# Perceiver block on one NeuronCore: all four P·V tiles of a batch in one slot, four buffers of transposed P, one of keys

## What is computed

```
ln = _ln(latents, g_l, b_l);  xn = _ln(x, g_x, b_x)          # latents 16x64x512, x = context 16x512x512
q = ln @ w_q
k, v = split(concat([xn, ln], axis=1) @ w_kv)                # 576 keys and values per batch
sim = einsum('bhid,bhjd->bhij', q * scale, k)                # 8 heads of 64
attn = softmax(where(mask, sim, -max))                       # P
out = einsum('bhij,bhjd->bhid', attn, v)                     # P·V
return _ln(out @ w_out, g_o, b_o)
```

## Time and profile before

| | us |
|---|---|
| three runs | 958.75, 959.94, 959.97 |
| median | 959.94 |
| the profiled execution | 958.88 |
| its span, first to last instruction | 957.1 |

### The profile page before, as it was taken

How to read it: one execution, slowest core, us unless ns; L and a number is a source line. 1 busy time by engine, 2 the same in 40 slices (tenths; PEclk the granted TensorE clock), 3 DMA queues, 4 the chain that set the end, 5 groups by cost and what they waited for, 6 DMA issues and landing times.

```text
span 957.1 us, 16824 instructions
## 1 busy us (share of the span) xinstructions
PE 942.2 (98%) x6400; PEld 777.4 (81%) x6400; DVE 730.1 (76%) x1512; ACT 522.4 (55%) x1088; POOL 142.7 (15%) x175
## 2 busy tenths in 40 slices
PE   9999999999999999999999999999999999999997
PEld 8778888888888888888888888776776778888885
DVE  6636577788787887886886854778898788999985
ACT  4535777777687777777776874623343422222221
POOL 6420101101201210111012010132231100000000
PEclk9999999999999999999999999999999999999999
DMA  6687657655675565676567535090004940000000
GB/s 223 167 280 209 200 135 192 158 130 157 166 185 131 163 152 154 155 196 149 129 147 181 157 106 161 12 242 2 1 1 118 247 121 12 11 12 12 12 12 23
DMA packets 119453, 120.07 MB, mean 125 GB/s; under 512 B 47430, under 2 KB 88070, under 8 KB 117324
## 3 DMA queue, kind: packets, MB, share of 16 engines
q1 hardware_dynamic: 111980, 93.30, 37.3%
q0 software_dynamic: 6816, 24.64, 8.3%
q10 hardware_dynamic: 576, 1.05, 0.3%
HBM read 89.04 MB, written 29.93 MB: 124 GB/s over the span
## 4 chain that ended last, share of the span: by engine, by line
PE 85%; DVE 6%; ACT 4%; DMA 2%; SPq 1%; issue 1%; POOL 0%; DVEq 0%; ACTq 0%; POOLq 0%
PE ps_banks L147 21%; PE ps_banks L148 21%; PE ps_banks L149 21%; PE ps_banks L473 6%; PE ps_banks L605 4%; PE ps_banks L686 3%; PE ps_banks L755 2%; PE ps_banks L756 2%; PE ps_banks L757 2%; SPq L132 1%; DMA sb_w_out_raw<-in_w_out 1%; DMA sb_wdn<-scratch_wdn 1%; PE ps_banks L486 1%; PE ps_banks L589 1%; PE ps_banks L651 1%
## 5 line engine op out<-in xcount | busy, mean ns | idle before, releaser
L147 PE MATMUL ps_banks<-sb_zT_hi,sb_wkv_hi 128*128 128x512 f32 x256 | 104.7, 409 | 0.0
L148 PE MATMUL ps_banks<-sb_wkv_lo,sb_zT_hi 128*128 128x512 f32 x256 | 100.4, 392 | 0.0
L147 PE MATMUL ps_banks<-sb_wkv_hi,sb_zT_hi 128*128 128x512 f32 x256 | 100.4, 392 | 0.0
L149 PE MATMUL ps_banks<-sb_zT_hi,sb_wkv_lo 128*128 128x512 f32 x256 | 100.3, 392 | 0.0
L149 PE MATMUL ps_banks<-sb_wkv_hi,sb_zT_lo 128*128 128x512 f32 x256 | 100.0, 391 | 0.0
L148 PE MATMUL ps_banks<-sb_zT_lo,sb_wkv_hi 128*128 128x512 f32 x256 | 99.9, 390 | 0.0
L987 DVE CUSTOM_DVE_ANT_0 sb_probs<-ps_banks,sb_maskbias 128x576 f32<-128x576 f32 x64 | 48.2, 754 | 41.5 <-PE ps_banks L149 39.9
L936 DVE TENSOR_TENSOR sb_kfull<-ps_banks,sb_rstd_row 128x512 f32<-128x512 f32 x64 | 44.2, 690 | 44.2 <-PE ps_banks L149 44.2
L1466 ACT ACTIVATE sb_kT_hi<-sb_kfull 128x512 fp32r<-128x512 f32 x64 | 40.5, 632 | 65.2 <-DVE sb_kfull L936 64.4
L147 PE MATMUL ps_banks<-sb_wgu,sb_z_hi 128*128 128x512 f32 (+1 forms) x192 | 74.0, 385 | 0.0
L148 PE MATMUL ps_banks<-sb_wgu,sb_z_hi 128*128 128x512 f32 (+1 forms) x192 | 72.1, 376 | 0.0
(11 more groups left out here) (275 smaller groups left out, 2520.8 us busy)
## 6 DMA issues: line engine op xcount, KB each, us to landing
sb_ctx<-in_ctx SPq DMA_DIRECT2D x16, 1024.0 KB, 6.4
sb_ctxT<-in_ctx_t SPq DMA_DIRECT2D x16, 1024.0 KB, 6.1
scratch_wgu<-sb_w_both POOLq DMA_DIRECT2D x22, 512.0 KB, 5.5
sb_wgu<-scratch_wgu SPq DMA_DIRECT2D x44, 256.0 KB, 5.0
sb_wdn<-scratch_wdn SPq DMA_DIRECT2D x8, 704.0 KB, 8.5
scratch_q<-sb_a_qk POOLq DMA_DIRECT2D x8, 512.0 KB, 6.6
sb_rstd_row<-scratch_rstd SPq DMA_DIRECT2D x16, 256.0 KB, 4.3
sb_qpack<-scratch_q SPq DMA_DIRECT2D x32, 128.0 KB, 6.2
```

Source lines behind the costliest of these rows:

```text
L147: e.matmul(o, wh, xh, start=i == 0, stop=False)
L148: e.matmul(o, wh, xl, start=False, stop=False)
L149: m = e.matmul(o, wl, xh, start=False, stop=i == n - 1)
```

## The change

- `weigh_v` of all four tiles of a batch stands in slot 3 of the next batch; slot 0 has none. In the last turn, b = 16, it is the same.
- Transposed P gets four buffers, one for each tile, in place of two: `p_main[n]` for the 512 context keys and `p_latent[n]` for the latents. `copy_p(b, n)` waits for `weigh_v(b - 1, n)` in place of the tile two before it. The ones in the latents' buffers are set four times at the start, not twice.
- `k_full` has one buffer. `scale_k` of a tile waits until `lo_of_k` of the tile ahead of it is done, not of the one before that. Both are DVE's.
- `w_q4` loses its own buffer: the rounded weights are written over `quant_w[3]` (`xn`, step 3's result). So step 3 of a job waits until the job ahead has been turned; before, the last step did.
- Two sets of statistics share their first tile with others, and two tiles of the self attention (`y[1]` and a gap of 2048 bytes) change places.

```
-                    if old and slot == 0:
-                        weigh_v(b - 1, 0)
-                        weigh_v(b - 1, 1)
                     if old and slot == 3:
-                        weigh_v(b - 1, 2)
-                        weigh_v(b - 1, 3)
+                        for n in range(C):
+                            weigh_v(b - 1, n)
...
+                        p = p_latent[n][:, r] if k == CS else p_main[n][:, k, r]
+                        m = e.matmul(o_space(r, n), value, p, start=k == CS, stop=k == CS - 1)
...
-                if idx >= 2:
-                    on.wait_ge(k_split, idx - 1)
-                e.tensor_tensor(k_full[n % 2][:, :], psum[:, bank, :], rstd_row[:, :], ALU.mult).then_inc(drained[bank])
+                if idx:
+                    on.wait_ge(k_split, idx)
+                e.tensor_tensor(k_full[:, :], psum[:, bank, :], rstd_row[:, :], ALU.mult).then_inc(drained[bank])
...
-                        if step == QUANT_STEPS - 1 and job:
+                        if step == 3 and job:
                             taken(("w", job - 1))
...
-                if idx >= 2:
-                    on.wait_ge(v_weighed, idx - 1)
-                copy(p_t[j][:, 0:CS, :].rearrange("p c n -> p (c n)"), psum[:, bank, :], drained[bank])
+                if b:
+                    on.wait_ge(v_weighed, C * (b - 1) + n + 1)
+                copy(p_main[n].rearrange("p c n -> p (c n)"), psum[:, bank, :], drained[bank])
...
+        w_q4 = quant_w[3]
-        y = [sb(stage_d, f"y{i}", [P, D]) for i in range(2)]
+        y = [sb(stage_d, "y0", [P, D]), None]
+        leave(2048)
...
-        leave(2048)
+        y[1] = sb(stage_d, "y1", [P, D])
```

More of the change, by code:

```diff
@@ L216, in perceiver @@
         lam = sb(ctx, "lam", [P, 8])
-        small_z = ln_small(ctx, "e", NT)
         small_o, small_y = ln_small(ctx, "lo", NT), ln_small(ctx, "ly", NT)
-        small_b = ln_small(ctx, "b", CS)
+        small_z = (small_y[0], sb(ctx, "e_mv", [P, NT, 2]), sb(ctx, "e_ve", [P, NT]), sb(ctx, "e_rstd", [P, NT]))
+        small_b = (small_o[0], sb(ctx, "b_mv", [P, CS, 2]), sb(ctx, "b_ve", [P, CS]), sb(ctx, "b_rstd", [P, CS]))
         rstd_b = sb(ctx, "rstd_b", [P, 2, CS])
@@ L260, in perceiver @@
         ctx_t = sb(stage_b, "ctxT", [P, C, S])
-        k_full = [sb(stage_b, f"kfull{i}", [P, S]) for i in range(2)]
+        k_full = sb(stage_b, "kfull", [P, S])
+        p_main = [None, None, sb(stage_b, "probsT2", [P, CS, P]), None]
         z_hi = [sb(stage_b, f"zT_hi{i}", [P, C, S], F32R) for i in range(2)]
@@ L269, in perceiver @@
         probs = [sb(stage_b, f"probs{i}", [P, S + LQ]) for i in range(2)]
-        p_t = [sb(stage_b, f"probsT{i}", [P, CS + 1, P]) for i in range(2)]
+        p_whole = [sb(stage_b, f"probsT{i}", [P, CS + 1, P]) for i in range(2)]
         mask_in = [sb(stage_b, f"mask{i}", [P, S], U8) for i in range(2)]
@@ L279, in perceiver @@
         w_in = [sb(stage_b, f"w_in{i}", [P, D]) for i in range(2)]
-        w_q4 = sb(stage_b, "w_q4", [P, D])
+        p_main[3] = sb(stage_b, "probsT3", [P, CS, P])
         w_both = sb(stage_b, "w_both", [P, 2, C, P], F32R)
@@ L283, in perceiver @@
         quant_w = quant_small(stage_b, "wq4", D)
+        w_q4 = quant_w[3]
         rstd_row = sb(stage_b, "rstd_row", [P, S])
+        p_latent = [sb(stage_b, f"probsT_l{i}", [P, P]) for i in (2, 3)]
+        p_main = [p[:, 0:CS, :] for p in p_whole] + [p[:, :, :] for p in p_main[2:]]
+        p_latent = [p[:, CS, :] for p in p_whole] + [p[:, :] for p in p_latent]
         stage_b.close()
@@ L592, in weigh_v @@
             def weigh_v(b, n):
-                i, j = b % 2, n % 2
+                i = b % 2
                 on.wait_ge(drained[took["p", b, n][0]], took["p", b, n][1])
@@ L604, in weigh_v @@
                         value = vl_pack[i][:, vs] if k == CS else v_sb[i][:, k, vs]
-                        m = e.matmul(o_space(r, n), value, p_t[j][:, k, r], start=k == CS, stop=k == CS - 1)
+                        p = p_latent[n][:, r] if k == CS else p_main[n][:, k, r]
+                        m = e.matmul(o_space(r, n), value, p, start=k == CS, stop=k == CS - 1)
                 m.then_inc(v_weighed)
@@ L933, in scale_k @@
                 on.wait_ge(w_folded, 2 * C)
-                if idx >= 2:
-                    on.wait_ge(k_split, idx - 1)
-                e.tensor_tensor(k_full[n % 2][:, :], psum[:, bank, :], rstd_row[:, :], ALU.mult).then_inc(drained[bank])
+                if idx:
+                    on.wait_ge(k_split, idx)
+                e.tensor_tensor(k_full[:, :], psum[:, bank, :], rstd_row[:, :], ALU.mult).then_inc(drained[bank])
             def lo_of_k(b, n):
-                split_lo(k_full[n % 2][:, :], k_hi[:, n, context_keys], k_lo[:, n, context_keys], k_hi_done, C * b + n + 1, k_split)
+                split_lo(k_full[:, :], k_hi[:, n, context_keys], k_lo[:, n, context_keys], k_hi_done, C * b + n + 1, k_split)
             def batch_stats(b):
@@ L1545, in hi_of_k @@
                     on.wait_ge(scored, C * (b - 1) + n + 1)
-                copy(k_hi[:, n, context_keys], k_full[n % 2][:, :], k_hi_done)
+                copy(k_hi[:, n, context_keys], k_full[:, :], k_hi_done)
             def copy_v(b, k):
@@ L1567, in copy_p @@
             def copy_p(b, n):
-                j, idx = n % 2, C * b + n
                 bank = taken(("p", b, n))
-                if idx >= 2:
-                    on.wait_ge(v_weighed, idx - 1)
-                copy(p_t[j][:, 0:CS, :].rearrange("p c n -> p (c n)"), psum[:, bank, :], drained[bank])
+                if b:
+                    on.wait_ge(v_weighed, C * (b - 1) + n + 1)
+                copy(p_main[n].rearrange("p c n -> p (c n)"), psum[:, bank, :], drained[bank])
             def copy_p_latents(b, *tiles):
@@ L1576, in copy_p_latents @@
                 for j, n in enumerate(tiles):
-                    if C * b + n >= 2:
-                        on.wait_ge(v_weighed, C * b + n - 1)
-                    m = e.activation(p_t[n % 2][0:LQ, CS, :], psum[0:LQ, bank, j * P:(j + 1) * P], ACT.Copy)
+                    if b:
+                        on.wait_ge(v_weighed, C * (b - 1) + n + 1)
+                    m = e.activation(p_latent[n][0:LQ, :], psum[0:LQ, bank, j * P:(j + 1) * P], ACT.Copy)
                 m.then_inc(drained[bank])
@@ L2017, in pool_program @@
                         zero_pack(e, 1)
-                        for i in range(2):
-                            e.memset(p_t[i][LQ:P, CS, :], 1.0).then_inc(p_zeroed)
-                        on.wait_ge(p_zeroed, 2)
+                        for p in p_latent:
+                            e.memset(p[LQ:P, :], 1.0).then_inc(p_zeroed)
+                        on.wait_ge(p_zeroed, C)
                     if b + 1 < NB and slot == 2:
```

## The result

| | before | after |
|---|---|---|
| median | 959.95 us (5 runs) | 963.52 us (5 runs) |
| range | 958.75 to 960.75 | 962.91 to 964.53 |
| the profiled execution, its span | 958.88, 957.1 | 963.19, 961.4 |

The change makes the kernel slower by 3.6 us: ratio 1.0042, 95% interval 1.0031 to 1.0053. The forecast was 960.4 with a range to 963.2; the time lies just above it.

What follows compares the result with a forecast made beforehand. TensorE's program was taken to bound the kernel, busy 942.2 of 957.1 us. Terms -4.2 - 0.3 + 3.3 + 0.9 + 0.8 = +0.5 us gave 960.4 us, own range 958.7 to 962.1, stated range 956.2 to 963.2.

Steps and rivals of the forecast that it cites:

- slot 0 against slot 3, 15 batches: Slot 0 loses 1.44 us of P·V, slot 3 gains 1.16: 0.28 us a batch, 4.2 us gained.
- batch 1, beyond that: P·V's 0.66 us wait in slot 0 goes; PE next meets tile 3's P, 1.75 us earlier, 0.3 more gained.
- even batches 4 to 14: Slot 1: tile 3's transposes wait for the turned weight's bank, drained by `lo_of_weight`; 3.3 us lost over six batches.
- odd batches 3 to 13: Slot 1: waits for banks drained by `copy_p` (tile 3's transposes) and `scale_k` (keys); some 0.9 us lost over six.
- last turn: P·V in slot 0 filled a wait, so nothing is saved and slot 3 grows: 0.8 us lost, at most 1.16.
- single keys buffer and the other edits: `scale_k` waiting for `lo_of_k`, step 3's earlier wait, P buffers, shared statistics, moved tiles: taken as nothing.
- The price of the edge: Starting and ending a separate P·V group in slot 0 costs 0.28 us a batch, which merging saves.
- the forecast's wait for `copy_p`: Slot 1 of odd batches: tile 3's transposes wait for tile 2's bank, 0.06 us in batch 9, 0.42 in batch 5.
- the forecast's worst: Each term at its worse bound (last turn 1.16, twelve batches 0.1 us more each): +2.1 us, 962.1 us.
- rival 2: Single keys buffer delays `scale_k` of slots 1 to 3 by 0.10 us on the path: 4.5 us more, 964.9; chance 0.11.
- (1): Even batches' waits do not come, as DVE gets ahead in slots 4 to 7: 956.2 us; chance 0.15.
- (3): A group's edge is one of tiling modes and stays, two tiles costing 1.44 us in slot 3: 964.6 us; chance 0.05.

Runs made afterwards that it cites:

- e1_split: Changed kernel with P·V of tiles 0 and 1 back in slot 0, tiles 2 and 3 in slot 3, other edits kept: 958.93 us, ratio 0.9991 to before.
- e3_z_early: Changed kernel with `lo_of_z` before the last rounding step on DVE in slot 7 of even batches from 2 on: 963.80 us.
- e5_all: Changed kernel with four reorderings on DVE and ACT, and P·V of tiles 0 and 1 back in slot 0 in the last turn: 956.47 us, ratio 0.9970.
- e7_odd: Changed kernel with `lo_of_z` earlier in slot 7 of even batches and `hi_of_weight` ahead of ACT's sums in slot 0 of odd batches: 960.72 us.
- e4_w_early: Changed kernel with `lo_of_weight` before the first two rounding steps on DVE in slot 0 of even batches: 961.18 us.

## Why the prediction was wrong

| step of the sum | forecast | traces before and after |
|---|---|---|
| slot 0 against slot 3, 15 batches | -4.2 | -3.9 |
| batch 1, beyond that | -0.3 | +0.7 |
| even batches 4 to 14 | +3.3 | +3.2 |
| odd batches 3 to 13 | +0.9 | +2.7 |
| last turn | +0.8 | +0.6 |
| single keys buffer and the other edits | 0 | 0 (e1_split) |
| sum | +0.5 | +3.3 |

Batch 2 loses another 0.1 us at its first key matmul, and batch 5 0.2 us at the keys of slot 2.

The price of the edge, the place and nearly the size of the even batches' wait, the last turn and the zero for the other edits held. (The 0.06 us from a drain's end to PE's start was read where an input ended; at the banks above it was 0.14 to 0.15.) The step that failed is the sentence that heads the losses: "each claim of slots 0 to 2 has to be set against the end of the work that drains its bank". It asks only for the banks. The first key matmul of a batch also has an input, `z_split`, and the order of PE after the change, printed above the prediction, shows that wait on that very row. DVE's row at 377.83, shown in the first section, put it 0.90 us ahead of its use. By the prediction's own method that gives 378.51 + 0.06 = 378.57 against 379.41 - 1.44 = 377.97, 0.60 us in batch 9, where I wrote 0.13; the traces say 0.48. The same omission turned batch 1 from a gain into a loss: I took tile 3's P as what PE would meet next there and did not look at the keys between. Odd batches and batch 1 make 1.8 + 1.0 = 2.8 us of error, and the median missed by 3.1. Nor were the 0.9 us that I did book for odd batches lost where I put them. In batch 5, where the size fitted (0.49 forecast, 0.54 lost), the loss too was the wait for `z_split`; the forecast's wait for `copy_p` stood behind it, and shows once the first is gone (e3_z_early, e5_all). That agreement was luck.

The range has a slip of its own. Its upper end is called the forecast's worst, 962.1, with half of rival 2's cost, and that is 962.1 + 2.25 = 964.4, not the 963.2 that was stated.

The second layer, the bank of slot 2 in odd batches, was within the words of that step, but its margin was never worked out. It cost 0.2 us of batch 5 in the changed kernel, because in the other odd batches the wait in slot 0 stood in front of it; it came up when that was removed.

Of the rivals, (1) was refuted by the waits themselves. (2) and (3), with 964.9 and 964.6, came nearer to the time than the forecast and had the wrong mechanism. Against (2) stand the trace of the changed kernel, which has no room for 0.10 us a tile of keys, and e1_split; against (3) the size of slot 3. A time near a rival's proves nothing for it.

## What to carry to other kernels

Work that stands between a product and its use is a cover. Before it is moved, list for every instruction between its old and its new place all semaphores that it waits for, inputs as well as buffers, each with its margin in the trace; a margin under what is moved is a loss. When such a wait is removed, look at the next one behind it before the gain is booked. And a merging that loses may be sound: here five moves, four of which are worth nothing without the merging, turned a loss of 3.6 us into a gain of 2.9.

## What the runs showed of the hardware

**A wait of PE costs more than its row says.** Matmuls overlap, and the bracket counts only from the end of the row before. In batch 9 of the changed kernel the first key matmul starts 0.54 us after the latents' transposes and its row has a wait of 0.26; in e5_all, without the wait, it starts 0.03 us after them (377.59 to 377.62). So the delay was 0.51 us, twice what is recorded. In batch 7 of e3_z_early a key matmul comes 0.20 us late and its row has no wait at all. The next one then follows after 0.34 us (320.78 to 321.12), where in e7_odd the same two are 0.23 apart. After transposes this last part isn't seen: there the second key matmul follows after 0.31 us without a wait and 0.33 with one.

**The clock falls in the last microseconds of some executions.** By the windows of PE (start and end, length, busy us and instructions, granted clock, DMA share, GB/s), after and then e3_z_early:

```profile
954.00:956.00 2.00, 0.89 (x4) 1.00 0.00 0
956.00:958.00 2.00, 2.00 (x10) 1.00 0.00 0
```

```profile
952.00:954.00 2.00, 0.59 (x5) 1.00 0.00 0
954.00:956.00 2.00, 2.00 (x7) 0.54 0.00 0
956.00:958.00 2.00, 2.00 (x7) 0.61 0.00 0
```

In both, PE idles for 0.34 us before its last four transposes and for 1.41 us behind them, waiting for `h_lo`. In one its last twelve matmuls go on at 2.4 GHz. In the other the clock falls to half, the level of 1.2 GHz: most of the twelve start 0.43 us apart in place of 0.23, and only the last two are 0.23 apart again. From the first to the last it takes 4.2 us in place of 2.7:

```profile
954.26 0.63 PE L764 MATMUL ps_banks<-sb_wdn,sb_h_lo 128*128 128x512 f32 x1
954.68 0.63 PE L762 MATMUL ps_banks<-sb_wdn,sb_h_hi 128*128 128x512 f32 x1
```

That 1.5 us is why e3_z_early's profile has the span of after, 961.4, although its loop ends 1.5 us earlier. Of the kernel before, 15 of 45 executions had a mean clock of 0.998, at a mean of 960.87 us against 959.28 at 1.00. The share was different from kernel to kernel (1 of 11 in e1_split, 8 of 12 in e4_w_early, 5 of 5 in e3_z_early). What decides it is open.
